# Whole quads of value sums in one visit, in the self-attention schedule of a three-layer decoder kernel

## What is computed

```python
q = (h @ Wq + bq).reshape(B, S, H, hd).transpose(0, 2, 1, 3)
...
scores = jnp.einsum('bhqd,bhkd->bhqk', q, k) / hd ** 0.5
scores = jnp.where(causal, scores, -jnp.inf)
attn = jax.nn.softmax(scores, axis=-1)
o = jnp.einsum('bhqk,bhkd->bhqd', attn, v)
```

## Time and profile before

| | |
|---|---|
| median of 3 runs | 1411.02 us (1407.18 to 1412.46) |
| the profiled execution's own time | 1407.71 us |
| its span | 1406.0 us |
| PE busy | 1300.1 us |
| DVE busy | 978.8 us |
| ACT busy | 643.6 us |
| POOL busy | 138.3 us |

### The profile page before, as it was taken

One profiled execution on the slowest core, in us unless ns is written; L12 is line 12 of the kernel. 1 busy time (PEld: TensorE's weight loads), 2 busy tenths in 40 slices (PEclk: granted clock), 3 DMA queues, 4 the chain that ended last, 5 costly groups with the idle time before them and its releaser, 6 DMA issues.

```text
span 1406.0 us, 18730 instructions
## 1 busy us (share of the span) xinstructions
PE 1300.1 (92%) x7463; PEld 958.5 (68%) x7463; DVE 978.8 (70%) x1412; ACT 643.6 (46%) x938; POOL 138.3 (10%) x217
## 2 busy tenths in 40 slices
PE   8786768999889999999999999999999999999997
PEld 6353436666655555456787888888888888888886
DVE  6998996798688888865756656555655556555567
ACT  5697563436347777785324233332322323232232
POOL 5000002000512333311000000000000000000000
PEclk9998889999889999999999999999999999999999
DMA  4000001002621122212000012110201102010001
GB/s 136 1 1 0 0 1 34 0 1 75 193 92 53 50 62 60 70 31 79 28 16 16 1 31 75 38 45 16 68 15 38 45 16 68 16 38 15 1 16 45
DMA packets 38583, 55.76 MB, mean 40 GB/s; under 512 B 8960, under 2 KB 23728, under 8 KB 38496
## 3 DMA queue, kind: packets, MB, share of 16 engines
q1 hardware_dynamic: 33312, 43.67, 10.3%
q0 software_dynamic: 3648, 10.09, 2.6%
q10 hardware_dynamic: 1536, 0.81, 0.2%
HBM read 43.73 MB, written 10.55 MB: 39 GB/s over the span
## 4 chain that ended last, share of the span: by engine, by line
PE 49%; DVE 3%; issue 0%; ACT 0%; DMA 0%; DVEq 0%; ACTq 0%
PE PS L2418 24%; PE PS L2431 23%; PE PS L122 1%; PE PS L114 0%; PE PS L2437 0%; DMA x_raw<-L_ffn_e_w 0%; PE PS L2216 0%; DVE OT_all L2550 0%; DVE r_st L2270 0%; DVE r_on L2287 0%; DVE x_mid L2543 0%; DVE x_mid L2541 0%; DVE r_on L2267 0%; PE PS L2450 0%; PE PS L2194 0%
## 5 line engine op out<-in xcount | busy, mean ns | idle before, releaser
L2418 PE MATMUL PS<-x_h,x_w 128*128 128x512 f32 x1536 | 400.8, 396 | 0.3 <-ACT x_bias L2492 0.3
L2490 ACT ACTIVATE x_g<-PS,x_bias 128x512 f32<-128x512 f32 x256 | 175.8, 687 | 486.7 <-PE PS L2418 486.6
L2431 PE MATMUL PS<-x_mid,x_w 128*128 128x512 f32 x1488 | 383.8, 393 | 0.0
L2418 PEld LDWEIGHTS PS<-x_h,x_w 128*128 128x128 f32 x1536 | 287.0, 188 | 65.9 <-ACT x_bias L2492 0.5
L2431 PEld LDWEIGHTS PS<-x_mid,x_w 128*128 128x128 f32 x1488 | 279.5, 188 | 64.1
L2541 DVE CAST x_mid<-x_g 128x512 fp32r<-128x512 f32 x256 | 109.1, 426 | 271.4 <-ACT x_g L2490 271.3
L2056 DVE TENSOR_REDUCE a_M<-PS 128x2 f32<-128x1024 f32 (+1 forms) x144 | 170.7, 1222 | 34.6 <-PE PS L1774 26.9
L2543 DVE TENSOR_TENSOR x_mid<-x_g,x_mid 128x512 fp32r<-128x512 f32 x256 | 177.3, 693 | 8.8
L1994 ACT ACTIVATE f_parts<-PS 128x512 f32<-128x512 f32 x224 | 121.1, 599 | 38.5 <-PE PS L1828 32.0
L1851 PE MATMUL PS<-f_parts,aV 128*32 128x256 f32 (+1 forms) x960 | 74.5, 391 | 0.0
L691 ACT ACTIVATE c_hot<-c_idxT,c_cid 128x1024 bf16<-128x1024 bf16 x65 | 70.2, 1138 | 7.6 <-PE PS L335 7.6
(11 more groups left out here) (361 smaller groups left out, 1610.5 us busy)
## 6 DMA issues: line engine op xcount, KB each, us to landing
x_raw<-L_ffn_e_w SPq DMA_DIRECT2D x32, 512.0 KB, 3.8
qk_parts<-f_parts SPq DMA_DIRECT2D x16, 512.0 KB, 3.4
x_wb<-route_w POOLq DMA_DIRECT2D x31, 256.0 KB, 3.5
aK<-qk_parts SPq DMA_DIRECT2D x96, 64.0 KB, 2.6
aQ<-qk_parts SPq DMA_DIRECT2D x96, 64.0 KB, 2.6
X<-x SPq DMA_DIRECT2D x4, 512.0 KB, 7.5
out<-X SPq DMA_DIRECT2D x4, 512.0 KB, 3.0
O<-itok_BxSx SPq DMA_DIRECT2D x2, 256.0 KB, 8.1
```

The lines of the kernel that those rows point to most:

```text
L2418: last = e.matmul(PS[:, f % 2, :], w1[n % 2][u][:, kt, f * P:(f + 1) * P], self.rows(v, k)[:, kt, :], start=m == 0 and kt == 0, stop=m == ...
L2431: last = e.matmul(PS[:, 2 + 2 * (it % 2) + d, :], w2[n % 2][v][:, f, d * P:(d + 1) * P], mid[u][:, f % RM, :], start=f == 0 and m == 0, st ...
L2490: e.activation(g[s % RG][:, :], PS[:, f % 2, :], ACT.Gelu, bias=b1[:, n, f:f + 1]).then_inc(A.sem, 1)
```

## The change

The two entries of `PV_AT` of quads 0, 1, 4, 5, 6, 7 and 8 are made equal: both halves are issued in one step, one behind the other. For quads 0, 4 and 6 it is the later of the two steps, for quads 1, 5, 7 and 8 the earlier. Nothing else is changed: instructions, buffers and semaphores are the same.

```diff
         TURN_AT, ROWS_AT = 16, (33, 1)
-        PV_AT = [(3, 4), (5, 6), (6,), (8, 8), (9, 10), (11, 12), (13, 14), (16, 17), (18, 19), (19,)]
+        PV_AT = [(4, 4), (5, 5), (6,), (8, 8), (10, 10), (11, 11), (14, 14), (16, 16), (18, 18), (19,)]
         O_AT = (15, 5)
```

## The result

| | before | changed |
|---|---|---|
| median of 6 runs | 1409.51 us (1406.55 to 1412.65) | 1420.14 us (1417.21 to 1423.02) |
| the profiled execution's own time | 1407.71 us | 1422.70 us |
| its span | 1406.0 us | 1421.0 us |

The changed kernel takes 1.0079 times as long, with a 95% interval of 1.006 to 1.0098. That is 10.6 us by the medians, where the sum said 9.2, and slower by over 0.5%.

What follows compares the result with a forecast made beforehand. PE sets the pace with little lead over DVE and ACT, joined by short rings. Six stretches gave 8.7 us, the first group 0.7, the last turn -0.14: +9.2 on 1411.02, so 1420.2 us; range 1409.5 to 1424.

Steps and rivals of the forecast that it cites:

- the sum: Whole kernel: six stretches at +1.45 us, first group +0.7, behind the last turn -0.14; together +9.2 us.
- The rings collect the saving: PE's time saved in light steps is lost to waits for DVE and ACT; a stretch grows 1.45 us.
- a visit: PE's switch from scores to sums and back: fixed cost 0.14 us; five of 15 go, 0.70 us a group.
- light step: A step left without sums: lasts 0.65 us where it lasted 1.24, so -0.59, but is filled by a ring's wait.
- The walk: One group followed from its turn by the rings' wait rules: +1.45 us a stretch, 1420.2 us in all; chance 0.60.
- unit 5: Behind light step 3: waits for unit 3's maximum and goes at 530.63 us, +0.12; had no wait before.
- the rule: DVE: a maximum lets the waiting unit go 1.28 us after the maximum's own start.
- step 9: Left without sums: step 10's second bank waits for ACT until 1.24 us after it began, losing the whole -0.59.
- The collected saving: Rival: PE alone sets the pace and each saved visit gives 0.14 to 0.16 us; -5.3 us, 1405.7; chance 0.12.
- Cancelling: Rival: shifts cancel within a group, only quad 7's +0.43 before unit 0 stays; +3.0 us, 1414.0; chance 0.22.
- The worse case: Rival: a ring's wait also delays ACT's copies; a stretch grows by over 1.8 us, above 1424; chance 0.06.
- the cover that I priced at nothing: DMA, POOL and buffer edges, taken not to get worse; a failing one would cost its wait alone.

Runs made afterwards that it cites:

- short_both: Kernel before and changed kernel, both with exponentials and maxima cut to 128 of 512 columns: stretches of 26.60 and 26.17 us, whole times 1389.64 and 1389.34 us.
- q0_alone: Kernel before with only quad 0 made whole, in step 4: a usual stretch of 29.38 us against 29.22 before.
- q4_alone: Kernel before with only quad 4 made whole, in step 10: a usual stretch of 29.65 us against 29.22 before.
- q5_alone: Kernel before with only quad 5 made whole, in step 11: a usual stretch of 29.56 us against 29.22 before.
- q7_alone: Kernel before with only quad 7 made whole, in step 16: a usual stretch of 29.65 us against 29.22 before.
- short_max_after: Changed kernel with the maxima alone cut to a quarter of their columns: a usual stretch of 28.28 us against 30.78 in the changed kernel.

## Why the prediction was right

*The rings collect the saving.* Shown. With DVE and ACT short the changed schedule is faster, by 0.43 us a stretch; with them at full length it is slower, by 1.56. The 0.14 us of a visit holds by the pair of short_both: 0.68 with the wait that is left, for 0.70. That quads 1 and 8 save no visit is in the same number. The forecast that PE would be busy 0.7 us less a stretch missed: it is 0.4, for the most part since a wait inside a listed group counts as busy (the group of units 8 and 9 takes 0.99 us for 0.76 before). The rows give a light step 0.57 less and not the 0.59 used, which would make each pair's saving 0.14 and not 0.16; nothing in the result turns on the 0.02.

*The walk.* From the turn, in shifts against before, forecast and measured: step 17 +0.43 and +0.43; unit 1 +0.43 and +0.44; step 1 +0.65 and +0.67; unit 4 +0.57 and +0.61; step 4 -0.05 and -0.04; unit 5 +0.12 and +0.26; step 9 +0.64 and +0.77; step 11 +1.09 and +1.22; unit 16 +1.29 and +1.43; turn +1.45 and +1.56. The one mis-sized term is unit 5, and its 0.14 stay to the end: the maximum that it waits for started 0.06 later than forecast, and the unit went 1.36 us behind that start where the rule had 1.28. In q0_alone it is 1.36 again; what makes the 0.08 isn't shown. Of the units named for new waits, 5, 16 and 17 have one, and unit 9 had one already, hidden in its weight load.

*The sum.* Six stretches were to give 8.7 us and gave 8.69, which is luck: the usual stretch grew by 1.56 and not 1.45, but two of the six of before were already long, 29.50 and 29.59. Here the prediction misread its rows. It said that the four stretches between the first and the last are within 0.03 us of the first; the turns are at 460.51 and 490.01, so the second takes 29.50. Its windows weren't cut at the turn. The six of the changed kernel have none such, at 30.74 to 30.80 (the last 30.79). In the second stretch of before an exponential of step 4 starts some 0.3 us later than in the others. It isn't a chance of one execution: all six kernels with quad 0 in steps 3 and 4 and full exponentials have it, and the other eight don't. Why isn't settled. The first group was priced at 0.7 and grew by 0.88, but in single profiles it is a weak measure: with quad 4 alone it grew by 0.79, with quad 0 alone it shrank by 0.30.

*The time.* 1420.2 us forecast and 1420.14 measured is luck as well: the sum was 1.4 us short, and it stood on a median before of 1411.02 us from three runs, which is 1409.51 with six.

*The two engines.* The prediction put one light step, step 9, on ACT and the others on DVE. q4_alone has ACT's wait alone, q0_alone and q5_alone DVE's alone, q7_alone the maximum of unit 0. All four held to 0.1 us.

*The rivals.* The collected saving falls by the time and by its own condition: it needed a unit less than 0.1 us late behind a light step, and units 5 and 16 wait 0.25 and 0.52. Cancelling falls with q7_alone and q4_alone. The worse case didn't come; no wait of PE's sums is in the changed trace. But the copy of bank 7 there ends at 454.01 us, 0.3 ahead of quad 3's sums at 454.32, and in short_max_after the sums wait for it, so the cover that I priced at nothing is a thin one.

*The switch and the sign.* The Trainium skill says that changing the tiling mode drains TensorE (TensorEngine Tiling (Array Packing), Key Properties). The runs agree in so far as a visit has a cost of its own, 0.14 us; how much of it is the drain they don't show. The Trainium skill also says that emptying PSUM may become the bottleneck once TensorE is faster (TensorEngine Tiling (Array Packing), PSUM Bottleneck). That decided the sign: with both engines short the changed schedule gains 0.43 us a stretch, at full length it loses 1.56.

## What to carry to other kernels

Where PE feeds two engines through rings of two or three banks, its work between two feeds is what spaces them; gathering it saves a switch (0.14 us here) and costs more if a step then gets shorter than the other engine's cycle (here 1.24 us for two exponentials through three banks, 1.13 to 1.28 for a maximum). Look for the steps that are already short, and spread filler work into them: half a quad moved into step 7 gave 0.4 us a stretch while it cost a visit more. And follow one period through with the rules of its waits before building; measure it by the period in the trace, not by the whole time, when the parts outside wander by more than the effect.

## What the runs showed that I had not expected

The parts outside the groups are much less steady than the groups. Over 14 profiled executions the first turn came at 400.4 to 404.5 us and the part behind the last turn took 798.4 to 800.7, although nearly all of its code is the same; the usual stretches of one execution lie within 0.1 us. And the effects of single quads nearly add up (1.68 us for 1.56), although each works through waits.
